# Cross-attention in a decoder layer: the norm and transposition of two key chunks moved into the fourth group's loop

## What is computed

```python
q = (hidden_states @ Wq + bq).reshape(b, s, 16, 128).transpose(0, 2, 1, 3)
k = (encoder_hidden_states @ Wk + bk).reshape(b, se, 4, 128).transpose(0, 2, 1, 3)
v = (encoder_hidden_states @ Wv + bv).reshape(b, se, 4, 128).transpose(0, 2, 1, 3)
k = repeat(k, 4, axis=1); v = repeat(v, 4, axis=1)
q = rmsnorm(q, qn_w);     k = rmsnorm(k, kn_w)
scores = einsum('bhsd,bhed->bhse', q, k) / sqrt(128) + mask
probs = softmax(scores)
out = einsum('bhse,bhed->bhsd', probs, v).transpose(0, 2, 1, 3).reshape(b, s, 16 * 128) @ Wo
x = layernorm(x + out)
```

## Time and profile before

| | us |
|---|---|
| median of 3 runs | 1500.41 (1497.96 to 1501.67) |
| the profiled execution | 1499.99 |
| its span in the trace | 1498.2 |

### The profile page before, as it was taken

One profiled execution on the slowest core, in us unless ns is written; L12 is line 12 of the kernel. 1 busy time (PEld: TensorE's weight loads), 2 busy tenths in 40 slices (PEclk: granted clock), 3 DMA queues, 4 the chain that ended last, 5 costly groups with the idle time before them and its releaser, 6 DMA issues. The chain is left out here.

```text
span 1498.2 us, 24718 instructions
## 1 busy us (share of the span) xinstructions
PE 1397.5 (93%) x8497; PEld 1175.5 (78%) x8497; DVE 868.1 (58%) x3018; ACT 712.3 (48%) x1877; POOL 610.1 (41%) x936
## 2 busy tenths in 40 slices
PE   7889999999987999999999999999999998399996
PEld 6678888887866788888888888888888887277874
DVE  3654343434346576667666766766676665843457
ACT  3655555556335444444444444444454445243346
POOL 1221111212116455455545544554555446264174
PEclk9999999999998999999999999999999999699998
DMA  6211121212434221222122121212221213475372
GB/s 199 91 34 54 58 77 47 78 34 68 143 124 119 58 58 46 64 59 57 46 62 55 40 71 48 67 37 64 59 58 46 65 39 107 174 229 165 117 256 103
DMA packets 70547, 126.56 MB, mean 84 GB/s; under 512 B 11835, under 2 KB 47007, under 8 KB 69528
## 3 DMA queue, kind: packets, MB, share of 16 engines
q1 hardware_dynamic: 65848, 110.04, 24.1%
q0 software_dynamic: 4576, 14.95, 3.5%
HBM read 93.50 MB, written 31.45 MB: 83 GB/s over the span
## 5 line engine op out<-in xcount | busy, mean ns | idle before, releaser
L1361 POOL TENSOR_TENSOR b_pcarry<-b_half 128x1 f32<-128x1 f32 x173 | 49.2, 285 | 369.3 <-DVE b_rinv L1224 345.9
L76 PE MATMUL bank<-b_kTh,b_q 128*100 128x362 f32 x512 | 171.4, 336 | 7.8 <-POOL b_q L1382 5.6
L1105 ACT ACTIVATE b_probs<-b_probs,b_nmax 100x361 f32<-100x361 f32 x256 | 151.9, 593 | 19.2 <-DVE b_nmax L1218 18.9
L1218 DVE CUSTOM_DVE_ANT_0 b_probs<-bank,b_mask 100x361 f32<-100x361 f32 x256 | 135.5, 530 | 42.8 <-issue 38.3
L1393 POOL TENSOR_SCALAR b_probs<-b_probs,b_rinv 100x361 f32<-100x361 f32 x256 | 147.6, 588 | 0.0
L1100 ACT ACTIVATE b_pTh<-bank 121x400 fp32r<-121x400 f32 x192 | 96.6, 504 | 101.4 <-PE bank L937 96.6
L1211 DVE TENSOR_TENSOR b_pTl<-bank,b_pTh 121x400 fp32r<-121x400 f32 x192 | 109.8, 572 | 56.8 <-ACT b_pTh L1100 56.8
L1153 ACT ACTIVATE b_oTh<-bank,b_bv 128x400 fp32r<-128x400 f32 x64 | 38.0, 594 | 211.1 <-PE bank L76 211.1
L937 PE MATMUL bank<-ident,b_probs 100*121 100x100 f32 x768 | 109.6, 265 | 4.4 <-POOL b_probs L1393 3.5
L436 ACT ACTIVATE a_probs<-a_probs,a_nmax 100x100 f32<-100x100 f32 x256 | 93.1, 366 | 40.4 <-DVE a_nmax L555 40.3
L937 PEld LDWEIGHTS bank<-ident,b_probs 100*121 100x121 f32 x768 | 107.0, 185 | 6.6 <-POOL b_probs L1393 4.4
(11 more groups left out here) (256 smaller groups left out, 3810.2 us busy)
## 6 DMA issues: line engine op xcount, KB each, us to landing
q_d<-a_qb SPq DMA_DIRECT2D x64, 200.0 KB, 2.3
b_q_raw<-q_d SPq DMA_DIRECT2D x64, 200.0 KB, 2.4
b_q_raw<-rs_d SPq DMA_DIRECT2D x64, 200.0 KB, 3.4
b_ctxr<-in_ctxT SPq DMA_DIRECT2D x48, 242.0 KB, 4.6
y_d<-c_y SPq DMA_DIRECT2D x32, 256.0 KB, 3.4
c_Eraw<-in_expert_w SPq DMA_DIRECT2D x10, 512.0 KB, 7.5
a_stage<-in_Wq SPq DMA_DIRECT2D x4, 1024.0 KB, 5.1
stage<-in_Wo SPq DMA_DIRECT2D x8, 512.0 KB, 4.6
```

What stands on the lines that cost most here:

```text
L76: mm = eng.matmul(out, lhsT=l(c), rhs=r(c), start=first and k == 0, stop=last and k == n - 1)
L1105: act.activation(p, p, ACT.Exp, scale=-1.0, bias=nmax[:, s % 2, h:h + 1], accum_out=psums[:, s % 2, h:h + 1]).then_inc(e_rdy, 1)
L1218: dve.tensor_tensor_reduce(out=probs[:, s % 2, h, 0:SE], in0=s_bank[h % 2][0:S, 0:SE], in1=mask_s[:], scale=-1.0, scalar=BIG, op0=ALU.add, ...
L1361: pool.tensor_tensor(pcarry[:, k:k + 1], half_s[:, 0:1], half_s[:, 0:1], ALU.add)
```

## The change

The list of each engine is reordered; no instruction is added or taken away. TensorE transposes chunk 1 in the fourth group's loop after the third quarter, and chunk 2 after the fourth head's scores, ahead of the fourth quarter; both stood behind the product with the values. VectorE norms chunks 1 and 2 in the first and second round of the fourth group's loop, where chunk 1 was normed between the two reciprocals at the loop's end and chunk 2 after the row normalisation. It takes their low halves right after the second reciprocal, ahead of the row normalisation and of the low half of the head's output, behind which they stood. ScalarE takes the high halves right after the fourth exponential, ahead of the head's output. GpSimd makes the reciprocal root of chunk 2 right after that of chunk 1, ahead of the row norm's root.

```diff
--- before.py
+++ after.py
@@ -1036,12 +1036,16 @@
                         if before:
                             transpose_probs(n - 1, (s + 3) % 4, h)
                         quarter(h)
+                        if s == 3 and h == 2 and not last:
+                            transpose_keys(j + 1, 1)
                         if s == 0 and h == 0 and routed(j):
                             transpose_x2(j - 2)
                         if s == 0 and h == 2 and routed(j):
                             logits(j - 2)
                     if now:
                         scores(j, s, 3, par)
+                    if s == 3 and not last:
+                        transpose_keys(j + 1, 2)
                     quarter(3)
                     if s == 0 and now and not first:
                         if routed(j):
@@ -1066,9 +1070,6 @@
                         values(j, 1)
                         values(j, 2)
                     if s == 3:
-                        if not last:
-                            transpose_keys(j + 1, 1)
-                            transpose_keys(j + 1, 2)
                         output(j, 1, range(2, XG))
                 if past:
                     output(j - 1, 3)
@@ -1144,6 +1145,9 @@
                     if now:
                         queries_hi(n + 1)
                         exponent(j, s, 3)
+                    if s == 3 and not last:
+                        keys_hi(j + 1, 1, 1 - par)
+                        keys_hi(j + 1, 2, 1 - par)
                     if first:
                         for k in range(2):
                             split_hi(KV_PIECES + 2 * s + k)
@@ -1158,10 +1162,8 @@
                     if s == 0 and now and not first:
                         for c in range(KC):
                             values_hi(j, c)
-                    if s in (2, 3) and not last:
-                        keys_hi(j + 1, s - 2, 1 - par)
-                    if s == 3 and not last:
-                        keys_hi(j + 1, 2, 1 - par)
+                    if s == 2 and not last:
+                        keys_hi(j + 1, 0, 1 - par)
                 if past:
                     x2_transposed(B - 1)
             over_batches(act, body)
@@ -1261,15 +1263,20 @@
                             keys_lo(j + 1, 0, 1 - par)
                         if before:
                             probs_lo(n - 1, h)
+                        if s == 3 and h < 2 and not last:
+                            key_norm(j + 1, h + 1)
                     if s == 0 and routed(j):
                         keep_logits(j - 2)
                     if now:
                         queries(n + 1)
                         masked(j, s, 3)
                         invert_sums(j, s, 0)
-                        if s in (2, 3) and not last:
-                            key_norm(j + 1, s - 2)
+                        if s == 2 and not last:
+                            key_norm(j + 1, 0)
                         invert_sums(j, s, 2)
+                    if s == 3 and not last:
+                        keys_lo(j + 1, 1, 1 - par)
+                        keys_lo(j + 1, 2, 1 - par)
                     if first:
                         for k in range(2):
                             split_lo(KV_PIECES + 2 * s + k)
@@ -1281,8 +1288,6 @@
                         key_squares(j + 1, 2)
                     if s == 3 and not first:
                         apply_norm(j - 1)
-                    if s == 3 and not last:
-                        key_norm(j + 1, 2)
                     if before:
                         kv = (s + 3) % 4
                         dve.wait_ge(o_hi, n)
@@ -1292,9 +1297,6 @@
                     if s == 0 and now and not first:
                         values_lo(j, 0)
                         values_lo(j, 1)
-                    if s == 3 and not last:
-                        keys_lo(j + 1, 1, 1 - par)
-                        keys_lo(j + 1, 2, 1 - par)
                     if s == 3 and not first:
                         dve.wait_ge(x2_out, 16 * j)
                 if past:
@@ -1414,14 +1416,13 @@
                         expert_lo(1)
                     if not last:
                         key_rsqrt(j + 1, 1)
+                        key_rsqrt(j + 1, 2)
                 if not first:
                     pool.wait_ge(mv_set, j)
                     pool.tensor_tensor(rstd[:], mv[:, 1:2], ln_eps_s[0:S, :], ALU.add).then_inc(rstd_set, 1)
                     pool.wait_ge(rstd_set, 2 * j - 1)
                     pool.tensor_tensor(rstd[:], rstd[:], half_s[0:S, 0:1], ALU.pow).then_inc(rstd_set, 1)
                 if not past:
-                    if not last:
-                        key_rsqrt(j + 1, 2)
                     normalise(j, 3)
                     if last:
                         for n in range(2, 2 * PRE):
```

## The result

| | before | after |
|---|---|---|
| median of the runs, us | 1501.04 (6 runs, 1497.82 to 1505.51) | 1488.60 (6 runs, 1485.23 to 1493.14) |
| ratio, 95% interval | | 0.9934 (0.9912 to 0.9956) |
| span of the profiled execution | 1498.2 | 1487.4 |
| period from batch to batch | 51.19 | 50.53 |

A forecast was written before the change was run, and what follows sets the result against it. TensorE was taken as the bound, busy 50.35 of 51.20 us a batch. 14 batches at 0.6 us plus 0.9 for the first give 9.3 us: 1500.4 to 1491.1 us, range 1488.5 to 1497.

The forecast's parts named there:

- The stalls of TensorE: End of group 4: time at the key transpositions of chunks 1 and 2 falls from 1.33 to 0.84 us a batch.
- The second gap: Before the next batch's first scores: 0.18 us a batch, read as waiting for VectorE's last key low halves, goes.
- VectorE's lag: Group 4's loop: two added norms make the fourth head's masking and first pair's reciprocal 0.70 us later, bounds 0.6 and 0.94.
- its chain: GpSimd's normalising, awaited by next batch's first transposition of probabilities: 3.56 us undisturbed, about 0.3 more with row normalisation.
- Rival A: Batch start: GpSimd keeps the shared port through its second pair; gain 0.3 us a batch, 1495.3 us; chance 0.17.
- B: VectorE is 0.94 us or more later in group 4; gain 0.25 us a batch, 1496.0 to 1497 us; chance 0.12.
- The store: VectorE's first masking waits for normalised rows landing at 812.0 to 813.2; covered by 0.1 to 1.3 us, costed at nothing.
- The first batch: Its 1.81 us stall goes, but VectorE is later there; half taken, 0.9 us, bounds 0 and 1.8.

The follow-up runs named there:

- The first experiment: Changed kernel with VectorE's low halves of key chunks 1 and 2 put back behind row normalisation and head output's low half: period 51.82 us against 50.53.
- two moves worth 0.06 us together: Changed kernel with row normalisation behind the head output's low half and the wait for its store moved to next batch's group 2: period 50.47 us, 1493.99 us.

## Why the prediction was right

Right in direction and mechanism; the sum was a little short, 9.3 us for a span that is 10.8 shorter. That the median still fell inside the range, by 0.1 us, is partly luck: a second measurement gave 1489.82, and the traced terms, 10.5 us (below), would give 1489.9.

- **The stalls of TensorE.** 0.72 us a batch was the most. With the transpositions of probabilities at 806.19, which is 810.79 on the clock of the earlier trace rows, 0.73 is what came. Both sets of transpositions cost 0.34 us (0.35 in the sum), the restart after each 0.07.
- **The second gap.** Read from 0.10 us between the end of the low half and the scores, in a place to which no view gave a releaser. The first experiment bears it out, though it made the wait longer and didn't take apart the 0.18 us themselves.
- **VectorE's lag.** 0.70 us forecast, 0.68 measured. Counting by starts and not by durations was the right choice.
- **GpSimd.** Forecast: its chain ends at 810.55 undisturbed and about 810.85 with the row normalisation in it. Measured: 806.10, which is 810.70. The row normalisation started at 804.58 (809.2 forecast, 809.18 measured), took 0.54 us and lengthened the second pair by 0.19, where I had 0.3. This is the term that was mis-sized: 0.12 us a batch was set aside for TensorE's wait, and 0.07 was lost. It makes 0.655 us instead of 0.6, over 14 batches 0.8 us. Rival A's handover didn't occur there, and B's larger lag neither.
- **The rule of the Trainium skill** (SBUF — State Buffer, "SBUF: two separate sides") that one engine holds the shared port pair for a whole instruction left the handover open. The trace agrees in that one engine's step waits for the other's (0.56 us for a step of 0.19 in the earlier trace rows). Who comes in between two of GpSimd's steps the traces answer in both ways. In the steady batches VectorE started at 804.58, between the low half of the queries and the second pair, and took its 0.54 us. In the last batch of the changed kernel it came in between two scaling steps (0.53 us, the pair 1.40 instead of 1.11, shown above). In a second execution of the same kernel, at the same place, it did not:

```profile
1251.93 1.11 POOL L1395 TENSOR_SCALAR b_probs<-b_probs,b_rinv 100x361 f32<-100x361 f32 x2
1252.44 0.87 DVE L1355 TENSOR_SCALAR b_y<-b_y,b_mv,b_rstd 100x512 f32<-100x512 f32 x1
```

So the kind of the steps doesn't decide it, and the prediction's argument against rival A, that the next step was of another kind, isn't borne out. That A stayed away in the steady batches is shown; why is not.

- **The store.** 2.3 us to landing were taken from another transfer of the same size; the wait ended 2.97 after the issue. The issue came at 809.75, at the early end of the 809.7 to 810.9 forecast, so the masking, at 812.72, was still inside the 812.0 to 813.2: one error made up for the other, which is luck. The cover named, 0.1 to 1.3 us, was 0.7.
- **The first batch.** 0.9 us forecast, 1.3 measured: at 480.5 both traces agree within 0.03 us, and the next batch's scores start at 503.58 instead of 504.91.

```profile
503.58 0.41 PE L76 MATMUL bank<-b_kTh,b_q 128*100 128x362 f32 x1 [1.20 <-DVE b_Wol L1175]
```

TensorE now waits 1.20 us there for the splitting of Wo, which the stall of 1.81 us in the earlier trace rows had hidden.

So 1.3 + 14 x 0.655 = 10.5 us of the span's 10.8. The traces show just that up to the last batch: a scores product there starts at 1235.86 instead of 1246.36. Behind it the two executions differ by more than the change. The changed kernel ran from 1226 to 1246 at a granted clock of 0.91, the one before at 1.00 in the corresponding 1236 to 1256 (four transpositions of probabilities take 0.98 us at 1238.34, where 0.57 is usual), and the lead fell to 9.44 us (1245.59 for 1255.03); it is 10.8 at the end. The remaining 0.3 us are the balance of that, and no effect of the change is shown in them. The medians differ by 12.4 us, which the interval of the ratio (6.6 to 13.2 us) covers.

## What to carry to other kernels

Where one engine is busy 98 per cent of a period, its order is its time: look for each place at which it waits for a step that another engine could have taken earlier, and find room in that engine's idle time, not only a place in its list. Then follow the displaced steps to the next thing that TensorE waits for, here GpSimd's normalising and the landing of a store; the change ended within 0.1 us of the one and 0.7 us of the other, and each was reached by one more step in the wrong place. Check the last pass of a loop by itself, since other work stands there: two moves worth 0.06 us together in each batch cost some 7 us in the last.

## What the hardware did that I had not expected

- VectorE's row normalisation, 0.53 us by itself, took 8.58 us beside four large two-input steps of GpSimd in a row (9.30 us). It did not get in between two of them, in three kernels. Beside two short scaling steps it took 0.93 us, and 1.30 in the kernel before. In the last batch of the changed kernel it took 0.53 in one execution and 0.87 in another, at the same place: the outcome isn't fixed by the program.
- VectorE's wait for the store of 200 KB ended 2.97 and 2.99 us after the issue in two kernels, with loads issued right behind it; the median time to landing of a store of the same size elsewhere in the kernel is 2.3. Whether the loads make the difference isn't shown.
